# A mixture-of-experts kernel on one core: the normalised row is added to each expert's output instead of once in combine, and combine's scaling and stores move between engines

## What is computed

```python
x = x + graph_layer(layernorm(x), ...)            # h in the kernel
y = layernorm(x)
top_w, top_e = softmax(top_k(y @ gate_w + gate_b, 2))
sel = relu(y @ w1[e] + b1[e]) @ w2[e] + b2[e]     # for the two chosen e
z = y + sum(top_w * sel)
out = x + layernorm(z) * gamma + beta
```

## Time and profile before

| | |
|---|---|
| median of 3 executions | 2766.34 us (2762.56 to 2767.82) |
| the profiled execution, its own time | 2769.09 us |
| its span in the trace | 2767.1 us |
| from first to last scatter of experts' slots | about 2241 to 2666 us of the span |
| combine | about 2670 to 2767 us of the span |
| TensorE busy over the span | 2215.0 us (80%) |
| GpSimd busy over the span | 1788.6 us (65%) |
| VectorE busy over the span | 966.5 us (35%) |
| ScalarE busy over the span | 654.1 us (24%) |

### The profile page before, as it was taken

One profiled execution on the slowest core, in us unless ns is written; L12 is line 12 of the kernel. 1 busy time (PEld: TensorE's weight loads), 2 busy tenths in 40 slices (PEclk: granted clock), 3 DMA queues, 4 the chain that ended last, 5 costly groups with the idle time before them and its releaser, 6 DMA issues. The chain is left out here.

```text
span 2767.1 us, 41429 instructions
## 1 busy us (share of the span) xinstructions
PE 2215.0 (80%) x11549; PEld 1842.4 (67%) x11550; DVE 966.5 (35%) x2172; ACT 654.1 (24%) x1539; POOL 1788.6 (65%) x1887
## 2 busy tenths in 40 slices
PE   1779999999999888887776767567566589999987
PEld 0568787777777767665565546446444479999975
DVE  6743324233233322221321212112112733333347
ACT  2532323223222222111111010000000323323255
POOL 0557767777777777777777777777775045555544
PEclk9999999999999999998898889878777799999998
DMA  6544433444444444434343433333333632222245
GB/s 206 171 151 120 131 109 117 128 123 141 118 120 124 132 120 120 121 116 133 108 120 116 121 115 106 109 112 110 106 104 79 247 138 70 69 70 70 70 141 215
DMA packets 146277, 338.71 MB, mean 122 GB/s; under 512 B 36674, under 2 KB 56290, under 8 KB 146051
## 3 DMA queue, kind: packets, MB, share of 16 engines
q0 software_dynamic: 89296, 245.33, 30.2%
q1 hardware_dynamic: 39311, 59.54, 6.3%
q10 hardware_dynamic: 17588, 32.88, 3.6%
HBM read 292.84 MB, written 47.97 MB: 123 GB/s over the span
## 5 line engine op out<-in xcount | busy, mean ns | idle before, releaser
L1052 POOL DMA_INDIRECT rows<-feat,srcT x1540 | 1464.1, 951 | 502.2 <-issue 442.8
L1255 PE MATMUL psW<-rows,S 128*128 x3920 | 1055.3, 430 | 347.8 <-SPq L1023 319.1
L1255 PEld LDWEIGHTS psW<-rows,S 128*128 128x128 f32 x3920 | 834.4, 217 | 564.3 <-issue 429.5
L1127 DVE TENSOR_TENSOR S<-psHere,coefS 128x896 f32<-128x896 f32 x280 | 301.4, 1090 | 1305.7 <-PE psW L1255 1297.6
L1315 ACT COPY z<-psW 128x512 f32<-128x512 f32 x196 | 114.9, 586 | 1386.7 <-PE psW L1255 1386.1
L1221 PE MATMUL psG<-wb,zT 128*128 128x256 f32 (+1 forms) x1600 | 353.5, 379 | 0.0
L1221 PEld LDWEIGHTS psG<-wb,zT 128*128 128x128 f32 (+1 forms) x1600 | 300.6, 188 | 44.7
L1706 PE MATMUL psH<-xT,w1x 128*128 128x128 f32 x1840 | 227.0, 277 | 0.3
L1657 POOL DMA_INDIRECT expert_rows<-os,at_rows x114 | 113.9, 1000 | 171.6 <-DVE os L1765 171.6
L1706 PEld LDWEIGHTS psH<-xT,w1x 128*128 128x128 f32 x1840 | 216.7, 193 | 2.0 <-issue 1.9
L1715 PE MATMUL psO<-w2s,hT 128*128 x912 | 215.7, 379 | 0.0
(11 more groups left out here) (281 smaller groups left out, 1418.8 us busy)
## 6 DMA issues: line engine op xcount, KB each, us to landing
rows<-feat,srcT POOLq DMA_INDIRECT x1568, 2.8
g<-expert_rows SPq DMA_DIRECT2D x24, 512.0 KB, 5.7
w1s<-in_L_ffn_w SPq DMA_DIRECT2D x8, 1024.0 KB, 10.1
w2s<-in_L_ffn_w SPq DMA_DIRECT2D x16, 512.0 KB, 10.1
feat<-rows SPq DMA_DIRECT2D x24, 256.0 KB, 3.0
fts<-feat ACTq DMA_DIRECT2D x24, 256.0 KB, 2.9
h<-in_x ACTq DMA_DIRECT2D x24, 256.0 KB
y_rows<-y ACTq DMA_DIRECT2D x24, 256.0 KB
```

The source lines that it names most:

```text
L1052: e.indirect_dma_start(rows[:, j % RB * H:(j % RB + 1) * H], None, d.feat, bass.IndirectOffsetOnAxis(ap=srcT[:, j:j + 1], axis=0)).then_in ...
L1127: e.tensor_tensor(S[h0 + h][:, :].rearrange("p (s b n) -> p s b n", s=U, b=B), both[:, h * U:(h + 1) * U, :].unsqueeze(2).to_broadcast([P, ...
L1255: last = e.matmul(psW[:, bass.ds(bank[u], H)], S[h][:, u * ZC:(u + 1) * ZC], rows[:, bass.ds(slot[u], H)], start=False, stop=True, skip_gr ...
```

## The change

1. **Graph layer:** `mean` and `rstd` and their two copies per tile are gone.
2. **Experts:** three new buffers `xb`. VectorE's new `plus_b2` adds b2 to the fetched row of slot n + 2 ahead of slot n's output; the output is then the product plus `xb`. `fetch(n)` now waits for the `plus_b2` of slot n - 3 instead of its transposes. As the weights add up to 1, the weighted sum in combine then already holds `y`.
3. **Combine, TensorE and ScalarE:** no `y`, no identity product: eight records per tile instead of twelve. HK is 13 instead of 14 (one more `hi` load).
4. **Combine, the output:** VectorE finishes only half 0 of each tile. Half 1 is multiplied by `rs` on ScalarE (`scaled_half`, in its turn t for tile t - 3, placed between the diagonals of tile t and the deviation of tile t - 2) and has `hb` added on GpSimd (`shifted(t, 1)`).
5. **Combine, the stores:** SyncE issues them, in one stream with the loads: `load(t)`, then `rows_out(t - 5)`, which waits for both halves.

```diff
-HK = 14
+HK = 13
@@ graph_layer, vector
-                ch.add(e.tensor_copy(mean[0:Q, bass.ds(t2, 2)], mv[0:Q, :, 0]))
...
-                e.tensor_copy(rstd[0:Q, bass.ds(t2, 2)], r)
@@ experts, gpsimd
             def fetch(n):
                 if n >= XS:
-                    e.wait_ge(s_xt, n - XS + 1)
+                    e.wait_ge(s_xb, n - XS + 1)
@@ experts, vector
+            def plus_b2(q, ex):
+                e.tensor_tensor(xb[q][:, :], xs[q][:, :], b2b[:, bass.ds(ex * H, H)], ALU.add).then_inc(s_xb, 1)
             ex = load_experts(e, 0, regs[0:2])
             for k in range(2):
                 copy_x(k, k, False)
                 copy_w1(k, ex[k])
             e.wait_ge(s_b2, 16)
+            for k in range(2):
+                plus_b2(k, ex[k])
...
                     copy_x(n + 2, k, True)
                     copy_w1(k, ex[2 + j])
+                    if later(i) or j >= 1:
+                        e.wait_ge(s_oc, SB * i + j)
+                    plus_b2((j + 2) % XS, ex[2 + j])
                     if later(i) or j >= 2:
                         e.wait_ge(s_out[k], 16 * (SB // 2 * i + j // 2))
+                    e.wait_ge(s_xb, n + 1)
                     e.wait_ge(s_o, n + 1)
-                    e.tensor_tensor(os_[k][:, :], psO[k][:, 0:H], b2b[:, bass.ds(ex[j] * H, H)], ALU.add).then_inc(s_oc, 1)
+                    e.tensor_tensor(os_[k][:, :], psO[k][:, 0:H], xb[j % XS][:, :], ALU.add).then_inc(s_oc, 1)
@@ combine, sync
-            for t in range(D, NT2):
-                e.wait_ge(s_hb, t - D + 1)
-                e.wait_ge(s_y, t - D + 1)
-                e.wait_ge(s_sum, t - D + 1)
-                load(t)
+            def rows_out(t):
+                k, n = t % D, nodes_of(t)
+                e.wait_ge(s_o, t + 1)
+                e.wait_ge(s_og, t + 1)
+                e.dma_start(pairs_of(out, t, n), o[k][0:n, :]).then_inc(s_st[k], 16)
+            for t in range(D, NT2 + D):
+                if t < NT2:
+                    e.wait_ge(s_hb, t - D + 1)
+                    e.wait_ge(s_sum, t - D + 1)
+                    load(t)
+                rows_out(t - D)
+            for k in range(D):
+                e.wait_ge(s_st[k], 16 * len(range(k, NT2, D)))
@@ combine, scalar (rows_and_diagonals becomes diagonals)
-                rows_here(e, t)
-                for m in M:
-                    last = e.activation(y[k][:, part(m)], rows_of(t)[:, part(m)], ACT.Identity, ...)
-                last.then_inc(s_y, 1)
...
-            for t in range(NT2 + LAG):
+            def scaled_half(t):
+                k = t % D
+                e.wait_ge(s_a, t + 1)
+                e.wait_ge(s_rs, t + 1)
+                e.activation(a[k][:, part(1)], a[k][:, part(1)], ACT.Copy, scale=rs[k][:, 1:2]).then_inc(s_as, 1)
+            for t in range(NT2 + LAG + 1):
                 if t < NT2:
-                    rows_and_diagonals(t)
-                if t >= LAG:
+                    diagonals(t)
+                if t >= LAG + 1:
+                    scaled_half(t - LAG - 1)
+                if LAG <= t < NT2 + LAG:
                     deviation(t - LAG)
@@ combine, tensor
-                        e.matmul(ps..., dg..., g..., start=(j == 0), stop=False)
-                    last = e.matmul(ps[k][:, part(m)], ident[:, :], y[k][:, part(m)], start=False, stop=True)
+                        last = e.matmul(ps..., dg..., g..., start=(j == 0), stop=(j == K - 1))
@@ combine, gpsimd
-            def rows_out(t):   # issued the store
+            def shifted(t, m):
+                k = t % D
+                e.wait_ge(s_hb, t + 1)
+                e.wait_ge(s_as, t + 1)
+                if t >= D:
+                    e.wait_ge(s_st[k], 16 * (t // D))
+                e.tensor_tensor(o[k][:, part(m)], a[k][:, part(m)], hb[k][:, part(m)], ALU.add).then_inc(s_og, 1)
+            for t in range(NT2 + LAG):
                 if t < NT2:
                     with_beta(t)
-                if t >= LAG + 1:
-                    rows_out(t - LAG - 1)
+                if t >= LAG:
+                    shifted(t - LAG, 1)
@@ combine, vector (the memset of eps stays, the two operations on nmr go)
             def scaled(t):
                 e.wait_ge(s_mv, t + 1)
+                if t >= D:
+                    e.wait_ge(s_og, t - D + 1)
...
-            def shifted(t):
+            def shifted(t, m):
...
-                for m in M:
-                    last = e.scalar_tensor_tensor(o..., a..., rs..., hb..., ALU.mult, ALU.add)
-                last.then_inc(s_o, 1)
+                e.scalar_tensor_tensor(o[k][:, part(m)], a[k][:, part(m)], rs[k][:, m:m + 1], hb[k][:, part(m)], ALU.mult, ALU.add).then_inc(s_o, 1)
```

More of the change, by code:

```diff
@@ L962, in _, with graph_layer @@
             e.tensor_scalar(ident[:, :], ident_i[:, :], 0.0, None, ALU.is_equal)
-def graph_layer(nc, d, a, ctl, pairs, room, wend, srcT, dstS, wgtS, coefS, ident, wb, lw, hb, gw, s_w, logit, choice, mean, rstd, rows, s_row):
+def graph_layer(nc, d, a, ctl, pairs, room, wend, srcT, dstS, wgtS, coefS, ident, wb, lw, hb, gw, s_w, logit, choice, rows, s_row):
     from contextlib import ExitStack
@@ L1066, in _ @@
             e.wait_ge(s_node, 2)
-            PER = 22
+            PER = 21
             e.sem_inc(s_dve, PER)
@@ L1623, in experts @@
         os_ = [sb(f"os{k}", [P, H]) for k in range(2)]
+        xb = [sb(f"xb{k}", [P, H]) for k in range(XS)]
         psX, psH, psO = ([pb(f"{n}{k}") for k in range(2)] for n in ("psX", "psH", "psO"))
@@ L1761, in slots, with combine @@
                     copy_w1(k, ex[2 + j])
+                    if later(i) or j >= 1:
+                        e.wait_ge(s_oc, SB * i + j)
+                    plus_b2((j + 2) % XS, ex[2 + j])
                     if later(i) or j >= 2:
                         e.wait_ge(s_out[k], 16 * (SB // 2 * i + j // 2))
+                    e.wait_ge(s_xb, n + 1)
                     e.wait_ge(s_o, n + 1)
-                    e.tensor_tensor(os_[k][:, :], psO[k][:, 0:H], b2b[:, bass.ds(ex[j] * H, H)], ALU.add).then_inc(s_oc, 1)
+                    e.tensor_tensor(os_[k][:, :], psO[k][:, 0:H], xb[j % XS][:, :], ALU.add).then_inc(s_oc, 1)
             turns(e, SLOTS // SB, slots)
-def combine(nc, d, kept, ident, mean, rstd, wgt, gamma, beta, out):
+def combine(nc, d, kept, ident, wgt, gamma, beta, out):
     from contextlib import ExitStack
@@ L1783, in combine @@
         gm, bt = sb("gm", [P, H]), sb("bt", [P, H])
-        nmr = sb("nmr", [P, NT])
         eps = sb("eps", [P, 1])
-        hi, hb, y, a, o = ([sb(f"{n}{k}", [P, 2 * H]) for k in range(D)] for n in ("hi", "hbt", "yc", "ac", "oc"))
+        hi, hb, a, o = ([sb(f"{n}{k}", [P, 2 * H]) for k in range(D)] for n in ("hi", "hbt", "ac", "oc"))
         g = [sb(f"g{k}", [P, 2 * K * H]) for k in range(D)]
@@ L1794, in combine @@
         s_hi, s_g, s_st = sems("hi"), sems("g"), sems("st")
-        (s_w, s_y, s_dg, s_sum, s_bn, s_mv, s_sd, s_rs, s_a, s_hb, s_o, s_n) = (ctx.enter_context(nc.semaphore(n)) for n in
-                                                         ("gb", "y", "diagonal", "sum", "bn", "mv", "sd", "rs", "a", "hb", "o", "nmr"))
+        (s_w, s_dg, s_sum, s_bn, s_mv, s_sd, s_rs, s_a, s_hb, s_o, s_og, s_as, s_n) = (ctx.enter_context(nc.semaphore(n)) for n in
+                                                         ("gb", "diagonal", "sum", "bn", "mv", "sd", "rs", "a", "hb", "o", "o_pool", "a_scaled", "eps"))
         two = d.two[0:DUMP, :].rearrange("(n k) f -> n (k f)", k=K)[1:NPAD + 1, :]
@@ L1871, in _ @@
                 e.wait_ge(s_g[k], 16 * (t // D + 1))
-                e.wait_ge(s_y, t + 1)
                 for m in M:
                     for j in range(K):
-                        e.matmul(ps[k][:, part(m)], dg[k][:, m * K + j, :], g[k][:, (m * K + j) * H:(m * K + j + 1) * H], start=(j == 0), stop=False)
-                    last = e.matmul(ps[k][:, part(m)], ident[:, :], y[k][:, part(m)], start=False, stop=True)
+                        last = e.matmul(ps[k][:, part(m)], dg[k][:, m * K + j, :], g[k][:, (m * K + j) * H:(m * K + j + 1) * H], start=(j == 0), stop=(j == K - 1))
                 last.then_inc(s_sum, 1)
@@ L1951, in _, with gnn @@
                 if t >= LAG:
-                    shifted(t - LAG)
-def gnn(nc, d, a, ident, sent, got, s_row, logit, choice, mean, rstd):
+                    shifted(t - LAG, 0)
+def gnn(nc, d, a, ident, sent, got, s_row, logit, choice):
     from contextlib import ExitStack
@@ L1991, in gnn @@
         wb, lw, hb, gw = sb("wb", [P, HC, B, H]), sb("lw", [P, HC, H]), sb("hb", [P, H]), sb("gw", [P, HC, X])
-        graph_layer(nc, d, a, ctl, pairs, room, wend, srcT, dstS, wgtS, coefS, ident, wb, lw, hb, gw, s_w, logit, choice, mean, rstd, rows, s_row)
+        graph_layer(nc, d, a, ctl, pairs, room, wend, srcT, dstS, wgtS, coefS, ident, wb, lw, hb, gw, s_w, logit, choice, rows, s_row)
 def program(nc, a, out):
@@ L2023, in program @@
```

(2 more changed lines are left out.)

26 lines of the change are left out of this document (6 added, 20 removed).

## The result

Six runs of each kernel on one chip: after 2773.65 us (median, 2771.81 to 2776.16), before 2765.15 us (2760.43 to 2767.82). The ratio is 1.0033 with a 95% interval of 1.0023 to 1.0043: 9.1 us slower (6.4 to 11.9; the medians themselves lie 8.5 apart), beyond the 0.2% that can be told from no change. The forecast was +3.6 us, 2769.9 us. The measured 2773.65 us lies above the forecast's own range (2766 to 2773) and inside the one that counts the slower rivals in (up to 2776.5); a loss beyond 0.2% had been given a chance of 0.40, no change that can be told 0.51.

What follows compares the result with a forecast made beforehand. TensorE bounds the experts, VectorE's time per tile combine, and load(24)'s issue the end. VectorE's start on tile 24 +0.55, finish -0.2, store +3.2: +3.6, 2769.9 us; range 2766 to 2773, with the slower rivals 2765 to 2776.5.

Steps and rivals of the forecast that it cites:

- What bounds it: End of combine: it hangs on when load(24) is issued, its 53-partition loads running on one of 16 DMA engines.
- Graph layer, -0.3: Graph layer: two small VectorE copies a tile and two memsets go, saving 0.3 us.
- Experts, +0.4: Experts: the additions are hidden behind VectorE's wait for TensorE; only the later fetch(3) costs, 0 to 1.1 us, taken as +0.4.
- Start of combine: First tiles of combine: tile 0 at the lower clock, tiles 1 and 2 at full clock; statistics of tile 2 start at 2681.0.
- Pace: Combine: a loop through ScalarE takes 5.75 us for two turns, 2.875 per tile (2.77 to 2.95), no better than 2.84.
- the clock (0.03): Rival, chance 0.03: TensorE's clock falls in combine because it idles 0.9 of 2.9 us; +16 us, 2786.
- the loads (0.20): Rival, chance 0.20: the loads' round trip sets combine's pace; with `g` landing after 6.0 us, 2771.3 to 2772.5.
- TensorE waiting for `g` in the middle: Combine: one of the listed signs that would show the forecast wrong; no size given.
- Issue of tile 24's `hi`: Combine, SyncE: `hi` of tile 24 is issued at 2736.85, 5.6 us later than before.
- From there to TensorE's start, 15.7 us: Tail: from issuing tile 24's `hi` to TensorE's start takes 15.7 us instead of 19.0, later stores standing behind in the ring.
- Last store, +3.2: End: the 53-partition store moves to SyncE and one DMA engine, 4.3 us; +3.6 less 0.4 for GpSimd's slower wake and issue.
- GpSimd blocks VectorE (0.10): Rival, chance 0.10: in combine GpSimd's addition blocks VectorE's half, up to 1.29 us a turn; at 3.2 a tile, +5.9, 2775.8.

Runs made afterwards that it cites:

- the diagonals ahead: The changed kernel with ScalarE building the diagonals of tile t + 1 in turn t, ahead of its half: ratio to before 1.0023, combine 97.54 us.
- stores back: The changed kernel with only the stores issued by GpSimd again, the split kept: ratio to before 1.0066, combine 102.54 us.
- the three versions of the changed kernel: The changed kernel with the last store cut 48 + 5 (1.0015), tile 24's loads cut too (0.9973), and diagonals also ahead of ScalarE's half (0.9965).
- before with loads in pieces: The kernel before with the loads of tile 24 alone cut in 48 + 5 partitions: ratio to before 0.9969, combine 87.55 us.

## Why the prediction was right, and where its sizes were off

The sign, the place (tile 24's loads and the last store) and the mechanism were as forecast; +3.6 us was too little, against +5.6 and +7.4 in the traces and +9.1 (6.4 to 11.9) timed. That even the traces come near it owes something to luck: terms that were too small (the experts, the start, the pace) stand beside a store that was priced too high. Step by step:

- **What bounds it: right.** The end hangs on one DMA engine's transfer of 53 partitions. Cutting them at 48 removes the wait for tile 24 in all four kernels it was tried on, the pace being what it was.
- **Graph layer, -0.3:** not seen. Up to the first fetch the traces differ by 2.7 us in after's favour, against the medians; that stage varies too much between executions.
- **Experts, +0.4: mis-sized, +1.6.** The late third fetch costs what was forecast (+0.34 and +0.50). The longer gap at every twelfth slot, +1.2, was not foreseen; I had set everything after the start to nothing because VectorE waits there.
- **Start of combine: mis-sized.** Statistics of tile 2 should have come 11.2 us after the first `g`; they came at 12.05 (before 13.94). Tile 1 had been put at full clock; but after's clock was still 0.50 over 2673:2677 and 0.79 on the mean of 2677:2679, and tile 1 came 2.3 us after tile 0, where less than 2.0 had been put. From there the delay of 0.9 stays in.
- **Pace: right in its regular part, mis-sized on the whole.** 5.67 us for two turns against 5.75, through the loop that was written down; the diagonals ahead take it away. The mean from turn 2 to 20 is 2.99 a tile, more than the 2.95 that was allowed. Missed was the irregular part: nine pairs from turn 2 to turn 20 take 53.75 us against a forecast of 51.75 and an allowance of 0.25. Of that 1.5 lies in the first pair, at the lower clock, and 1.0 in the pairs of turns 14 to 18, waiting for `g`, less 0.5 in the others. Two rivals thus came in part: the clock (0.03) and the loads (0.20). TensorE waiting for `g` in the middle had been named as a sign of being wrong, and it did so at five tiles of the second half, by 0.4 to 2.2 us; `g` had been expected to land in near 5 us, and from 42 us after the first `g` on it took 5.5 to 6.4.
- **Issue of tile 24's `hi`: mis-sized.** 8.0 us later than before, counted from the first `g`, against 5.5: about the 0.9 and the 1.75 of the two points above.
- **From there to TensorE's start, 15.7 us: right,** 15.4, and for the reason given: the stores issued after these loads landed behind them (9.0 and 7.5 us), and with the stores back on GpSimd it is 18.2. The first product of tile 24 is 4.4 us later than before instead of 2.2. The tile takes 3.35 instead of the forecast 3.74; VectorE to the last piece 5.93, forecast 6.0.
- **Last store, +3.2: right in kind, mis-sized, +2.1.** The data take longer than forecast (5.5 us, not 4.3), but the end comes 0.8 us after them and not 2.9. I had priced the transfer and forgotten that GpSimd's queue has its own cost at the end.
- **GpSimd blocks VectorE (0.10):** only 0.3 us where they meet (0.78 for 0.48), and off the loop. With the stores back on GpSimd it comes in full, 3.3 us at a time.

Summed for the first pair of traces: TensorE's last start +4.4, its tile -2.1 (3.38 us to VectorE's start, before 5.50), VectorE to the last piece -0.3, the store +2.1, the experts +1.6: +5.7, read as +5.6. Open remain: 1.4 to 1.7 us of combine that come and go between executions of the changed kernel; the 1.7 to 3.5 between the traces and the timed +9.1 (on chip C, too, the timed differences of the three versions of the changed kernel lie 0.4 to 2.8 us above those of their traces, that of before with loads in pieces 0.6 to 1.2, so something may be lost ahead of the first fetch; no run shows it); and what of the edit lengthens the experts.

## What to carry to other kernels

When work is taken off the engine that sets the pace, follow the new order of every queue through one full turn: the halved work came back as a loop through ScalarE, whose order alone was worth 4 us. Then ask what the end hangs on: here it was neither engine but a transfer of 53 partitions, and cutting it at 48 took some 9 us off both kernels, as much as the whole change cost. And look at odd shapes of transfer again whenever they change queue.

## What the runs showed of the hardware

- A two-operand VectorE operation that starts just after a GpSimd operation can be held for the whole of GpSimd's unbroken run: 0.48 us of work lasted 3.82, across three additions and a store issue ("stores back", four times). Where GpSimd had gaps (after) it lasted 0.78.
- The end of the program follows 0.8 us after the last data of a store by SyncE (all seven traces), and 2.9 us after that of one by GpSimd's queue (all seven).
- A transfer of 53 partitions from SyncE moves at 20 to 25 GB/s, loads and stores alike; stores of 48 and of 5 partitions together move the same 106 KB in 0.8 us. Stores issued behind such loads by SyncE took 9.0 and 7.5 us to land in place of 2.0. The Trainium skill (page "DMA: Bandwidth & Descriptors", section "Why a DMA increments its semaphore by 16 and not by 1") has the rule, the largest number up to 16 that divides the slowest dimension: 1 for 53, 16 for 48. The runs agree: the cut took 7.8 to 9.8 us off combine for the loads and 4.6 off the end for the store.
- TensorE's granted clock fell to 0.50 after waits of 1.93 and 2.22 us in combine of after. It did not after every such wait: it stayed at 1.00 after one of 1.94 us at the same tile in "stores back", and after one of 1.93 us for `g` later in after.
